# Moving half of the low-part subtractions of the third layer's weights from GpSimd to VectorE, one part behind its sums

## What is computed

```python
x_q = x[:, Q_START:Q_END, :]
routing = softmax(x_q.mean(axis=1) @ router_W.T + router_b)
base = x @ W.T + b
t = einsum('bsd,erd->bser', x, A)
lora = einsum('bser,eor,be->bso', t, B, routing) * 2.0
x = layernorm(x + base + lora)
```

## Time and profile before

| | |
|---|---|
| runs | median 1810.24 us of 3 (1807.33 to 1810.25) |
| profiled execution | 1806.38 us, its span 1804.6 us |
| mean granted TensorE clock | 0.973 |
| TensorE busy | 1714.7 us (95%) |
| VectorE, ScalarE, GpSimd busy | 1069.0, 654.3, 437.0 us |

### The profile page before, as it was taken

The page is one execution under the profiler, slowest core; times in us unless marked ns, Lnnn a source line. Parts: engine busy times, 40 slices in busy tenths (PEclk is TensorE's granted clock), DMA queues, the critical chain, the costliest instruction groups (busy, mean ns, idle before and its releaser), DMA issues.

```text
span 1804.6 us, 23292 instructions
## 1 busy us (share of the span) xinstructions
PE 1714.7 (95%) x8154; PEld 1378.5 (76%) x8154; DVE 1069.0 (59%) x2049; ACT 654.3 (36%) x967; POOL 437.0 (24%) x380
## 2 busy tenths in 40 slices
PE   5999999999999999998879999999699899999998
PEld 4788888888888888887656666667578688787886
DVE  5433443345555555566377777777667676766733
ACT  2433333333333333322234545545333333423321
POOL 3111111100000000000166777773222122211200
PEclk9999999999999999999869999999699999999999
DMA  6223333323333333323031000002445456455321
GB/s 246 98 101 117 114 120 119 115 102 118 113 110 113 110 113 113 115 95 105 27 144 40 1 1 1 1 8 94 155 156 198 146 186 217 165 176 185 137 94 59
DMA packets 81541, 199.76 MB, mean 111 GB/s; under 512 B 9746, under 2 KB 26130, under 8 KB 81170
## 3 DMA queue, kind: packets, MB, share of 16 engines
q1 hardware_dynamic: 60690, 129.07, 21.1%
q10 hardware_dynamic: 20736, 69.22, 9.6%
HBM read 125.89 MB, written 72.35 MB: 110 GB/s over the span
## 4 chain that ended last, share of the span: by engine, by line
PE 86%; DVE 4%; issue 3%; DMA 2%; ACT 2%; POOL 1%; SPq 0%; ACTq 0%; POOLq 0%; DVEq 0%
PE ps L671 18%; PE ps L673 18%; PE ps L672 18%; PE ps L848 6%; PE ps L793 3%; PE ps L685 3%; PE ps L730 2%; PE ps L839 2%; PE ps L840 2%; PE ps L838 2%; PE ps L799 2%; PE ps L732 1%; PE ps L731 1%; PE ps L754 1%; PE ps L816 1%
## 5 line engine op out<-in xcount | busy, mean ns | idle before, releaser
L671 PE MATMUL ps<-wall_x,x_hi 128*128 128x512 f32 x1008 | 401.9, 399 | 10.2 <-DVE wall_x L1316 5.3
L673 PE MATMUL ps<-wall_x,x_lo 128*128 128x512 f32 x1008 | 396.8, 394 | 0.0
L672 PE MATMUL ps<-wall_x,x_hi 128*128 128x512 f32 x1008 | 396.4, 393 | 0.0
L1894 POOL TENSOR_TENSOR rstd<-var_eps,minus_half 128x1 f32<-128x1 f32 x96 | 77.0, 802 | 928.9 <-DVE minus_mean L1351 921.9
L1342 DVE BATCH_NORM_STATS2 stats<-row 128x6 f32<-128x512 f32 x192 | 133.0, 694 | 181.2 <-ACT row L1025 176.8
L671 PEld LDWEIGHTS ps<-wall_x,x_hi 128*128 128x128 f32 x1008 | 191.8, 190 | 53.4 <-issue 10.3
L673 PEld LDWEIGHTS ps<-wall_x,x_lo 128*128 128x128 f32 x1008 | 191.7, 190 | 41.3
L672 PEld LDWEIGHTS ps<-wall_x,x_hi 128*128 128x128 f32 x1008 | 192.2, 191 | 38.8
L671 PE MATMUL ps<-wall_y,x_hi 128*128 128x512 f32 x512 | 202.5, 396 | 0.0
L673 PE MATMUL ps<-wall_y,x_lo 128*128 128x512 f32 x512 | 199.7, 390 | 0.0
L672 PE MATMUL ps<-wall_y,x_hi 128*128 128x512 f32 x512 | 199.3, 389 | 0.0
(11 more groups left out here) (244 smaller groups left out, 2940.0 us busy)
## 6 DMA issues: line engine op xcount, KB each, us to landing
x_scratch<-row ACTq DMA_DIRECT2D x64, 512.0 KB, 2.7
x_in<-x_scratch SPq DMA_DIRECT2D x64, 512.0 KB, 3.6
w_in<-in_w_t SPq DMA_DIRECT2D x96, 256.0 KB, 2.8
out<-row ACTq DMA_DIRECT2D x32, 512.0 KB, 2.6
x_in<-in_x_t SPq DMA_DIRECT2D x29, 512.0 KB, 3.4
cx<-x_scratch SPq DMA_DIRECT2D x24, 512.0 KB, 3.9
x_scratch<-cx ACTq DMA_DIRECT2D x24, 512.0 KB, 2.7
w_more<-in_w_t SPq DMA_DIRECT2D x32, 256.0 KB, 3.0
```

What stands on the lines that cost most here:

```text
L671: pe.matmul(bank, hi[:, k], wall[:, k, 0, cols], start=(k == 0), stop=False)
L672: pe.matmul(bank, hi[:, k], wall[:, k, 1, cols], start=False, stop=False)
L673: return pe.matmul(bank, lo[:, k], wall[:, k, 0, cols], start=False, stop=(k == KC - 1))
L1894: pool.tensor_tensor(rstd[:, i:i + 1], var_eps[:, i:i + 1], minus_half[:, 0:1], ALU.pow)\
```

## The change

GpSimd makes no low parts any more. VectorE makes all of them, each one part behind its sums: after the sum of part i it makes the low part of i - 1, and after the last sum also the last. As `a_lo` of the next row block keeps its place right behind the sum of an even part, it now stands ahead of the low part of the odd part before. One semaphore counts all low parts, so `low_parts` is one wait in place of two.

```diff
         def low_parts(eng, n):
-            if n < BATCHES * PARTS:
-                at_least(eng, w_lo_ready, n + 1)
-            else:
-                eng.wait_ge(w_lo_ready, BATCHES * PARTS + (n - BATCHES * PARTS) // 2 + 1)
-                at_least(eng, w_lo_pool, (n - BATCHES * PARTS + 1) // 2)
+            at_least(eng, w_lo_ready, n + 1)
...
                     if i == 0 and n > BATCHES * PARTS:
                         split_a(n // 2)
                     weight_sum(n + i)
-                    if i % 2 == 0:
-                        if i + 2 < PARTS:
-                            split_a((n + i) // 2 + 1)
+                    if i % 2 == 0 and i + 2 < PARTS:
+                        split_a((n + i) // 2 + 1)
+                    if i > 0:
+                        weight_lo(n + i - 1)
+                    if i == PARTS - 1:
                         weight_lo(n + i)
...
-            def weight_lo(n):
-                b, k, o, _ = part_place(n)
-                cols = slice(o * HALF, (o + 1) * HALF)
-                pool.wait_ge(w_hi_ready, n + 1)
-                pool.tensor_tensor(walls[b][:, k, 1, cols], w_place(n), walls[b][:, k, 0, cols].bitcast(F32),
-                                   ALU.subtract).then_inc(w_lo_pool, 1)
...
                 if b == 0:
-                    for i in range(1, PARTS, 2):
-                        weight_lo(n + i)
-                        if i == 3:
-                            root_c(c + 1)
+                    root_c(c + 1)
                     root(p)
                     root(p + 1)
...
-                    for i in PART_STEP[b].get(j, ()):
-                        if i % 2:
-                            weight_lo(n + PARTS + i)
```

More of the change, by code:

```diff
@@ L351, in build @@
         w_diag, w_product, w_summed = sem("w_diag"), sem("w_product"), sem("w_summed")
-        w_hi_ready, w_lo_ready, w_lo_pool = sem("w_hi_ready"), sem("w_lo_ready"), sem("w_lo_pool")
+        w_hi_ready, w_lo_ready = sem("w_hi_ready"), sem("w_lo_ready")
         y_turned, y_hi_ready, y_lo_ready = sem("y_turned"), sem("y_hi_ready"), sem("y_lo_ready")
```

## The result

The changed kernel takes 1825.39 us (median of 4 runs, 1821.67 to 1828.29) beside 1810.24 us (4 runs, 1807.33 to 1810.65): ratio 1.0089, 95% interval 1.0072 to 1.0106. It is slower, by 15.2 us. Its profiled execution took 1825.34 us, its span 1823.6 us. Every ratio in this text sets the runs of a kernel against runs of the kernel before from the same round; it is not the quotient of two medians, from which it differs by up to 0.002. The medians of the kernel before in the later rounds were 1806.75 us (A to D), 1807.73 (E to H) and 1808.25 (I and J).

What follows compares the result with a forecast made beforehand. The bound was taken as a loop through `a_in` loads, its period nearly that of TensorE's own work. Terms 6.1 + 2.8 + 2.9 + 2.9 + 1.5 = 16.2 us on 1806.4, plus 3.8 to the median, gave 1826; range 1815 to 1838.

Steps and rivals of the forecast that it cites:

- The order decides, not the work: On VectorE, the odd low part would wait behind `a_lo` for an `a_in` load and hold back the next `a_in`.
- One row block per turn, 1.85 us + L: Loop of loads: a turn serves one row block, not two, taking 1.85 us plus L, the `a_in` landing time.
- The sign that was to speak against it: Prediction would be wrong if `a_in` loads of two row blocks were still under way at once in each turn.
- First build: Late first low part plus four turns, 22.8 against 18.9 us, 0.3 off: +6.1 us, bounds +1.9 and +10.4.
- the first step: First build: part 1's low part, now behind `residual`, the diagonal, part 2's sum and `a_lo`, comes 2.5 us later.
- Tile 7 of batch 0: Loop turns exceed TensorE's 2.7 us per row block; tile ends later by 1.7 to 3.8 us, taken as +2.8.
- Tiles 6 and 7 of the next two batches: VectorE held at `a_lo` of row block 4 delays TensorE, and the loop adds; 2.0 to 3.7 us, taken +2.9, twice.
- the loop: Tiles 6 and 7: the load loop, longer than TensorE's work, adds 1 to 1.5 us in row blocks 6 and 7.
- The clock: One stretch of lower TensorE clock behind new waits, in the changed stages: +1.5 us, bounds 0 and 5.
- The first rival (GpSimd off the path and off the port): Faster: quicker low parts and no waits for GpSimd save 4 to 5 us in the first build, 1805.5; chance 0.06.
- The second (room hides it): No change: VectorE's idle time in the first build hides the added low parts, 1810 to 1813 us; chance 0.08.
- The third (clock): Much slower: clock stays lower through most of the first build, 8 to 10 us more, 1836 us; chance 0.16.

Runs made afterwards that it cites:

- A: Changed kernel, with VectorE making the low part of i - 1 before `a_lo` of the next row block; 1810.73 us, ratio 1.0005.
- D: Changed kernel, with SyncE issuing each `a_in` load one weight earlier, VectorE's order untouched; 1801.73 us, ratio 0.996.
- E: Kernel before the change, with SyncE issuing each `a_in` load one weight earlier; 1800.07 us, ratio 0.9948.
- H: A, with the low part of part 7 made at the end of tile 6 in batches 2 and 3; 1808.67 us, ratio 1.0008.
- I: Changed kernel, with SyncE issuing each `a_in` load one weight later; 1850.71 us, ratio 1.0241.
- J: Kernel before, with VectorE's even low parts one part behind its sums, GpSimd keeping odd ones, `a_in` one weight earlier; 1801.23 us, ratio 0.9964.
- F: Changed kernel, with the low part ahead of `a_lo` and `a_in` issued one weight earlier; 1800.18 us, ratio 0.9939.
- G: Changed kernel, with part 1's low part ahead of `residual(c + 1)` in the first build; 1821.72 us, ratio 1.0064.
- C: Changed kernel, with each low part made right behind its own sum, all on VectorE; 1822.79 us, ratio 1.0071.

## Why the prediction was right

It named 1826 us, a range of 1815 to 1838 and a chance of 0.86 for slower; measured were 1825.39 us and a ratio of 1.0089. Point by point:

- *The order decides, not the work.* Shown from three sides: the same work in another order costs little or nothing (A, 1.0005), the same order with another load place costs nothing (D, 0.996), and with early loads the kernels with and without the 32 instructions on VectorE take the same (E, F).
- *One row block per turn, 1.85 us + L.* Shown on the chain: with L of 2.88, 3.09, 4.10 and 2.45 us this gives 4.7, 4.9, 6.0 and 4.3, and with 1.45 us for the `cx` and `cz` loads in the first two, 6.2, 6.4, 6.0 and 4.3; the turns took 6.06, 6.30, 5.86 and 4.53. The sign that was to speak against it, the `a_in` of two row blocks "still under way at once", did not come, but it was badly chosen: in the first build of the kernel before none were either (one landed at 1309.34, the next was issued at 1312.63). What that kernel had is a chain that runs through every second `a_in` only the earlier trace rows.
- *First build: forecast +6.1, measured +6.0.* Inside it the first step was forecast at 2.5 us; G puts it at 1.7, and in the trace the `a_hi` of row block 3 came 2.0 us later behind the first mark than before (15.8 for 13.9). The four turns took 22.75 us, forecast were 22.8, against 18.9 before. That they agree so well is luck in part: the last three landings were forecast as 3.9, 2.9 and 2.9 us and came as 3.09, 4.10 and 2.45, while all four together took the 12.5 us forecast. By TensorE's own account the 6.0 us are 3.9 more of waiting and 2.2 more lost to the lower clock (0.86 over the stage, 0.89 before). As the chain runs through the loads here and not through TensorE, the slow stretches only filled waits, as forecast: in the five microseconds from 1322, at a clock of 0.66, TensorE was busy throughout, and its wait behind them was the short one, 0.34 us.
- *Tile 7 of batch 0: forecast +2.8, measured +1.7*, the low bound. TensorE stood still there for 9.3 us where it had for 7.7, in five waits of 0.94 to 1.23 us behind the first of 3.81 (before, one of 2.15 and four of 0.5 or less). Its low stretch of the clock is in both profiles and weighs the same: 1.7 us before, and after 0.16 of 11 us, 1.8 (windows: length, busy PE, PEld, DVE, ACT, POOL, clock, DMA share, GB/s):

```profile
1428.00:1439.00 11.00, 10.02 (x36) 7.79 (x36) 6.21 (x14) 3.21 (x7) 0.00 (x0) 0.84 0.33 117
1551.00:1567.60 16.60, 15.70 (x56) 12.71 (x57) 9.91 (x21) 4.82 (x10) 0.00 (x0) 0.79 0.26 89
1567.60:1590.00 22.40, 20.40 (x93) 16.11 (x92) 16.90 (x34) 8.78 (x16) 0.55 (x1) 1.00 0.50 171
...
1701.00:1723.00 22.00, 19.65 (x84) 15.56 (x83) 16.49 (x33) 8.49 (x15) 0.55 (x1) 0.92 0.42 144
```

- *Tiles 6 and 7 of the next two batches: forecast +2.9 each, measured +5.3 and +4.1 in the one profile.* Here the term was mis-sized and part of the way to it was not the one described. The waits lie in tile 7 alone: 0.51 and 1.48 us in batch 1, 0.54 and 1.81 in batch 2, 2.0 and 2.35 together. The first of each pair is the one forecast, through `half_stats`, `normalise` and `a_hi` of row block 5; it was put at 1 to 2.2 us. The second is longer and was only called "the loop", at 1 to 1.5 us. VectorE's timeline at the start of tile 7 says why:

```profile
1570.93 0.68 DVE L1379 TENSOR_TENSOR wall_x<-w_more,wall_x 128x512 fp32r<-128x512 f32 x1
1571.53 0.69 DVE L1335 TENSOR_TENSOR row<-ps,bias 128x512 f32<-128x512 f32 x1
...
1573.36 1.21 DVE L1321 TENSOR_TENSOR x_lo<-ps,x_hi 128x1024 fp32r<-128x1024 f32 x1
1574.49 0.68 DVE L1373 TENSOR_TENSOR w_in<-ps,w_in 128x512 f32<-128x512 f32 x1
1576.49 0.29 DVE L1353 TENSOR_TENSOR a_lo<-a_in,a_hi 128x128 fp32r<-128x128 f32 x1 [1.32 <-ACT a_hi L1040]
1576.70 0.69 DVE L1379 TENSOR_TENSOR wall_x<-w_more,wall_x 128x512 fp32r<-128x512 f32 x1
```

  The low part of part 7 stands at 1576.70, behind `half_stats`, the cut of the next tile's input, part 8's sum and a wait for `a_hi`. It frees the slot for part 11, and behind that weight SyncE issues the `a_in` of row block 6 (at 1578.36, 8.5 us behind the start of the tile). That it is this low part H shows, if only from A and on one profile: made earlier, it took the second wait away in both batches.
- *The clock: forecast +1.5.* Tile 6 of batch 1 took 2.9 us more with the granted clock at 0.79 over 16.6 us (3.5 us by that), and no wait of TensorE there that was not in the kernel before: the one ahead of the stretch is 3.14 us in both. The kernel before and H kept their clock at 1.00 through this stage (20.6 us); the other nine lost 1.7 to 1.8 us to the clock there, the kernel after twice that. So how long this stage stays at the lower level looks like chance, and isn't put down to the change. Tile 7 of batch 2 had 0.92 over 22 us, 1.8 us, behind its new waits. This one looks like the change's: of the 24 tiles 7 of batches 1 and 2 in the twelve profiles, seven had such a stretch, and they are the seven in which TensorE waited longest in all. The stages without these two stretches give 6.0 + 1.7 + 2.4 + 2.3 = 12.4, which leaves 2.8 of the medians' 15.2 us to the clock. This is a remainder between one profile and the medians, not a measurement; it is more than 1.5 and within its bounds.
- *The sum* was right to 1 us in part by luck, because errors cancelled: tile 7 of batch 0 was put too high by 1.1, the two last terms by 1.1 (5.8 for 4.7), the clock too low by 1.3.
- *The first rival (GpSimd off the path and off the port)* has a true part: `a_lo` is back at 0.28 us. The Trainium skill (SBUF — State Buffer, Who interferes with whom) says that a VectorE instruction with two SBUF inputs and a GpSimd one that reads SBUF take turns; by that rule, the traces of both kernels agree, 1287 ns at most beside GpSimd's low parts and 293 without. No time won by it shows: `a_lo` lost 8.6 us in all, and VectorE waited right there. *The second (room hides it)* needed landings of 2 us; they took 2.45 to 4.10. It holds once the wait is out of the loop (A, D). *The third (clock)*: the first build was not at the lower level for most of its length (0.86 over it), and the 2.8 us above are not 10.

Why D and E are faster than the kernel before is argued, not isolated: the load of `a_in` was on that kernel's chain as well, and both orders take part of its landing out. The Trainium skill (DMA: Bandwidth & Descriptors, Rules for kernel authors) advises to issue a DMA early and to wait late. By that rule, D and I agree: for one weight load's place in the queue the ratio of the changed kernel, 1.0089, became 0.996 and 1.0241.

The fastest kernels found are E and F, 0.5 to 0.6% faster than the kernel before; the smallest edit is E, the load order alone. D, F and J can't be told from it.

## What to carry to other kernels

When an instruction is moved on an in-order engine, first write down which waits now stand ahead of it, and who waits for it: here low parts of 0.69 us each, moved behind a wait for one load, held back the next such load, and the kernel lost 15 us. An instruction that frees a slot belongs ahead of one that waits for a load, and a small load on which a chain depends belongs ahead of the large one in the queue. Leave a producer on another engine one step of lead before its result is read: the kernel that read it at once (C) was 12 us slower than the one that didn't (A).

## What the runs showed that was not expected

- A low part right behind its own sum leaves VectorE idle for 0.50 to 0.70 us. This is ScalarE's high part itself, 0.63 us, with 0.03 us or so ahead of it and behind it (C: the sum ends at 1566.95, the high part runs from 1566.99 to 1567.62, the low part starts at 1567.65). In a stage where VectorE was 80% busy before there was little room for it.
- A 64 KB `a_in` took 2.45, 2.88, 3.09, 3.89 and 4.10 us from issue to landing in one build, against a forecast of 2.8 to 3.9.
- A wait of 3.14 us on TensorE was followed by a granted clock of 1.00 in the kernel before and of 0.79 over 16.6 us in the kernel after, at the same place, and mostly by one of 0.92 over the stage in the others. One profile of a stage is good to some 3 us, no better.
